# Query corner sums kept in PSUM, and a new order of DVE's steps in the attention units of a two-layer kernel

## The reference, cut to what matters

```python
q = rope(ln(x) @ Wq)        # 32 heads of 128
k = rope(ctx @ Wk)          # 8 heads of 128, four q heads share one
v = ctx @ Wv                # 8 heads of 128
s = 30 * tanh(q @ k.T * 0.0884 / 30)
w = softmax(where(mask, s, -1e30))
x = x + (w @ v) @ Wo
# rope(a) = a * cos + concat(-a2, a1) * sin, a1 and a2 the halves of 128
```

## Time and profile before

| what | us |
|---|---|
| median of 3 runs (lowest, highest) | 883.85 (883.29, 885.22) |
| the profiled execution, its own time | 885.6 |
| its span, first to last instruction | 883.8 |
| mean granted clock of PE | 0.986 |
| PE busy | 826.6 (94%) |
| DVE busy | 592.6 (67%) |
| ACT busy | 476.1 (54%) |
| POOL busy | 455.9 (52%) |

### The profile page before, as it was taken

How to read it: one execution, slowest core, us unless ns; L and a number is a source line. 1 busy time by engine, 2 the same in 40 slices (tenths; PEclk the granted TensorE clock), 3 DMA queues, 4 the chain that set the end, 5 groups by cost and what they waited for, 6 DMA issues and landing times.

```text
span 883.8 us, 12187 instructions
## 1 busy us (share of the span) xinstructions
PE 826.6 (94%) x4298; PEld 674.8 (76%) x4298; DVE 592.6 (67%) x1093; ACT 476.1 (54%) x1100; POOL 455.9 (52%) x341
## 2 busy tenths in 40 slices
PE   9999988689889988899888997999999999999998
PEld 7898866477667666677666775889998888888887
DVE  6873589667576785767857844647435766677894
ACT  6531334544555355543555523266778877877762
POOL 5564485755866768667686542011222432338442
PEclk9999999799999999999999998999999999999999
DMA  8364302302232222322221273000100110300002
GB/s 291 140 240 134 131 13 61 89 20 84 60 120 61 74 71 60 120 60 72 71 61 49 67 257 113 13 24 25 48 25 24 49 36 25 124 20 1 1 1 96
DMA packets 33245, 67.01 MB, mean 76 GB/s; under 512 B 5152, under 2 KB 8480, under 8 KB 32544
## 3 DMA queue, kind: packets, MB, share of 16 engines
q1 hardware_dynamic: 30640, 61.38, 22.3%
q10 hardware_dynamic: 2544, 4.85, 1.6%
HBM read 54.55 MB, written 11.67 MB: 75 GB/s over the span
## 4 chain that ended last, share of the span: by engine, by line
PE 52%; POOL 16%; DVE 14%; issue 10%; ACT 4%; DMA 4%; SPq 0%; DVEq 0%; POOLq 0%; ACTq 0%
PE PB L1790 10%; PE PB L1791 10%; PE PB L1792 10%; PE PB L2042 8%; PE PB L2057 3%; PE PB L1797 3%; PE PB L1827 2%; POOL WSl L1139 2%; POOL WVl L1139 2%; POOL W L1139 2%; DVE arena L1650 2%; POOL qb L1175 2%; DVE qb L1576 2%; POOL Eb L1195 2%; ACT arena L1312 2%
## 5 line engine op out<-in xcount | busy, mean ns | idle before, releaser
L1175 POOL TENSOR_TENSOR qb<-qb,arena 128x512 f32<-128x512 f32 x76 | 101.8, 1347 | 84.7 <-DVE arena L1583 44.3
L1476 DVE TENSOR_TENSOR xs<-xs,PB 128x512 f32<-128x512 f32 x111 | 74.1, 674 | 37.9 <-PE PB L1792 29.7
L1252 ACT ACTIVATE Oh<-PB 96x128 fp32r<-96x128 f32 (+2 forms) x236 | 79.3, 358 | 33.8 <-PE PB L1792 15.3
L1139 POOL TENSOR_TENSOR WVl<-stage,WVh 128x512 fp32r<-128x512 f32 (+1 forms) x25 | 37.4, 1513 | 70.7 <-ACT WVh L1252 64.3
L1790 PE MATMUL PB<-WVh,Oh 128*128 128x512 f32 x158 | 62.9, 398 | 5.6 <-POOL WVl L1139 5.3
L1827 PE MATMUL PB<-Th,WSh 128*128 128x512 f32 x112 | 45.7, 408 | 17.8 <-POOL WSl L1144 8.8
L1791 PE MATMUL PB<-WVl,Oh 128*128 128x512 f32 x158 | 61.6, 390 | 0.0
L1792 PE MATMUL PB<-WVh,Ol 128*128 128x512 f32 x158 | 61.6, 390 | 0.0
L1790 PE MATMUL PB<-W,Oh 128*128 128x512 f32 x142 | 56.5, 398 | 5.0 <-POOL W L1139 5.0
L1583 DVE TENSOR_TENSOR arena<-arena,ropeq 128x512 f32<-128x512 f32 x56 | 54.8, 979 | 4.3 <-ACT arena L1312 4.1
L1312 ACT ACTIVATE arena<-PB 64x512 f32<-64x512 f32 x28 | 16.5, 591 | 72.7 <-POOL qb L1175 70.5
(11 more groups left out here) (341 smaller groups left out, 2608.4 us busy)
## 6 DMA issues: line engine op xcount, KB each, us to landing
stage<-in_wq SPq DMA_DIRECT2D x44, 256.0 KB, 2.7
stage<-in_wo SPq DMA_DIRECT2D x44, 256.0 KB, 2.7
arena<-recs SPq DMA_DIRECT2D x32, 256.0 KB, 4.0
stage<-in_wk SPq DMA_DIRECT2D x12, 256.0 KB, 2.7
keys<-qb SPq DMA_DIRECT2D x12, 256.0 KB, 2.2
arena<-keys SPq DMA_DIRECT2D x6, 512.0 KB, 3.2
xs<-in_x SPq DMA_DIRECT2D x8, 256.0 KB, 6.9
ctx_hi<-cTh SPq DMA_DIRECT2D x1, 2048.0 KB, 8.8
```

The costliest lines, as they stand in the source:

```text
L1139: e.tensor_tensor(lo, src, hi.bitcast(f32), ALU.subtract).then_inc(s_wlo)
L1175: e.tensor_tensor(dst, dst, tmp, ALU.add).then_inc(s_radd)
L1252: return e.activation(dst, src, ACT.Copy)
L1476: e.tensor_tensor(xs[:, i, :], xs[:, i, :], PB[b][:, :], ALU.add).then_inc(free[b])
```

## The change

Three things are edited together.

1. The corner sums of the queries: `cmb` writes its sum into PSUM (bank 7 for t = 2 and 7, bank 0 for t = 3), not into `held`, and `rope p` becomes the three-instruction rope from PSUM that keys have. ACT's copies and the step `sin` are gone. Bank 7 is free only when rope 2 has read it. POOL's addition comes at the rope's place in the list.
2. The opening: the values' tiles go through `Eb` and `pTb` (`v_slot`), each two free for reuse when its transfer is done, no longer through `qb`; keys, values, q0 tiles, `pair(0)` and `pair(1)` stand in another order; the splits of wv0 1 stand ahead of the statistics.
3. The units: the addition of an output to x is a step of its own (`e0_add`), for units 0 to 13 moved behind output 2 and behind output 3. `sum0`, `norm0`, the splits of wp 2 and three of q0's tiles have other places in units 0 to 2, and `ctx_in` in unit 14.

```diff
 def e0(u, c, bank=None):
         stage("e0", u, c, bank=bank)
+        if u >= NU - 2:
+            e0_add(u, c)
...
     k0(5, 1)
     split("wk0", 7)
+    k0(6, 0)
+    spill_k(5, 1)
     vq(0)
-    spill_k(5, 1)
-    k0(6, 0)
+    spill_k(6, 0)
+    k0(6, 1)
     spill_v(0)
     split("wq0", 3)
     vq(1)
...
     spill_k(6, 1)
     k0(7, 0)
-    spill_v(2)
-    vq(3)
+    spill_v(1)
+    pair(0)
+    k0(7, 1)
     spill_k(7, 0)
...
+    for n in range(4):
+        vq(n + 2)
+        if n == 0:
+            spill_k(7, 1)
+            split("wq0", 2)
+        else:
+            spill_v(n + 1)
+        q0(0, n)
+        if n == 3:
+            q0(1, 1)
+    vq(6)
+    spill_v(5)
+    q0(1, 0)
+    q0(1, 3)
+    vq(7)
+    spill_v(6)
     spill_v(7)
     pair(1)
...
+        def added(*cs):
+            if u >= 2:
+                for c in cs:
+                    e0_add(u - 2, c)
...
+        if u == 1:
+            for n in range(2):
+                split("wp", u + 1, n)
         if u < 3:
             products(u, 1, 2)
-            query(0)
+        if u == 2:
+            step("sum0", 1)
+            step("sum0_out", 1)
+        if u == NU - 2:
+            step("ctx_in", 0)
         burst(u)
...
-        query(3)
-        if u in (1, *range(3, NU)):
+        if u >= 3:
             norm0(u - 1)
...
             products(u, 5)
             rope_p(u, 0)
-            sin(u, 0)
-        if u not in (1, 2):
+        if u >= 3:
             step("sum0", u)
             step("sum0_out", u)
         outputs(0)
-        if u >= NU - 2:
-            step("ctx_in", u - NU + 2)
-        query(1)
         if quad:
             products(u, 6, 3)
             rope_p(u, 1)
-        if 0 < u < NU - 3:
-            for n in range(2):
-                split("wp", u + 1, n)
+        if paired:
+            if u == 1:
+                step("pair", u + 1)
+            else:
+                for n in range(2):
+                    split("wp", u + 1, n)
         outputs(1)
         if quad:
             products(u, 7)
-            sin(u, 1)
-            query(2)
+            if u == 0:
+                q0(1, 2, bank=1)
             rope_p(u, 2)
-            sin(u, 2)
+        if u == 1:
+            norm0(0)
         if u == 2:
+            outputs(2)
+            added(0, 1)
             norm0(1)
-        if u in (1, 2):
-            step("sum0", u)
-            step("sum0_out", u)
-        outputs(2)
+            added(2)
+            step("sum0", 2)
+            step("sum0_out", 2)
+        if u != 2:
+            outputs(2)
+        if u == NU - 2:
+            step("ctx_in", 1)
+        if u != 2:
+            added(0, 1)
         if quad:
             products(u, 4)
             rope_p(u, 3)
-            sin(u, 3)
-        if 0 < u < NU - 3:
+        if u == 0:
+            step("sum0", 0)
+            step("sum0_out", 0)
+        if paired and u > 1:
             step("pair", u + 1)
         outputs(3)
+        added(*((3,) if u == 2 else (2, 3)))
...
# POOL: its addition for the queries
-                    if kind == "sin":
-                        pool.wait_ge(s_sin, 4 * k[0] + k[1] + 1)
+                    if k[0] == "p" and k[2] == 0:
+                        pool.wait_ge(s_sin, k[1] + 1)
                     else:
-                        pool.wait_ge(*read(*k))
+                        pool.wait_ge(*read(*product_of(*k)))
...
# ACT: rope p is removed
-                elif kind == "rope" and k[0] == "p":
...
-                    for r in range(2):
-                        last = e.activation(tmp_of(n)[64 * r:64 * r + 64], src[64 - 64 * r:128 - 64 * r], ACT.Copy, scale=-1.0)
-                    last.then_inc(s_swap)
...
# DVE
-                    cos = e.tensor_tensor(dst, src.rearrange("p (b t) -> p b t", b=8), ropeq[:, 0:1, :].broadcast_to([128, 8, 64]), ALU.mult)
...
-                    e.tensor_tensor(tmp, tmp, ropeq[:, 1:2, :].broadcast_to([128, 8, 64]), ALU.mult).then_inc(s_sin)
...
                     kept = held[{2: 1, 3: 6, 7: 5}[t]]
+                    to = PB[bank_of("p", u, 3 if t == 3 else 2)]
...
-                    e.tensor_tensor(kept, PB[bank_of("p", u, t)][:, :], kept, ALU.add).then_inc(s_cmb)
+                    e.tensor_tensor(to[:, :], PB[bank_of("p", u, t)][:, :], kept, ALU.add).then_inc(s_cmb)
```

More of the change, by code:

```diff
@@ L230, in plan @@
     stage("many")
+    split("wv0", 1, 0)
+    split("wv0", 1, 1)
     for i in HI:
@@ L846, in program @@
         s_spill = [sem(f"spill{n}") for n in range(8)]
+        s_vspill = [sem(f"vals_out{n}") for n in range(4)]
         s_kin, s_vin, s_cout, s_cin = [sem(f"keys_in{n}") for n in range(2)], sem("vals_in"), sem("ctx_out"), [sem(f"ctx_in{h}") for h in range(2)]
@@ L919, in products_of @@
             return x_block(((xTh, xTl), (Th, Tl))[kind], kk, hf)
-        spills = {st: n for n, st in enumerate(s[1:] for s in steps if s[0] == "spill")}
+        spills = {st: n for n, st in enumerate(s[1:] for s in steps if s[:2] == ("spill", "k"))}
         def spill_slot(*name):
@@ L934, in spill_done, with v_slot, v_sent, product_of @@
             return s_spill[n % 8], 16 * (n // 8 + 1)
+        def v_slot(i):
+            return (Eb, pTb)[i % 4 // 2][:, i % 2, :]
+        def v_sent(i):
+            return s_vspill[i % 4], 16 * (i // 4 + 1)
+        def product_of(kind, *k):
+            if kind != "p":
+                return (kind, *k)
+            u, t = k
+            return "p", u, (2, 5, 2, 1)[t]
         def tmp_of(n):
@@ L1165, in gpsimd_program @@
                     e.tensor_tensor(lo, wk0_1, hi.bitcast(f32), ALU.subtract).then_inc(s_k1lo)
-                elif kind == "sin" or kind == "rope" and k[0] != "p":
-                    name = ("p", *k) if kind == "sin" else tuple(k)
-                    n = ropes[name]
-                    dst = rope_place(*name)
+                elif kind == "rope":
+                    n = ropes[tuple(k)]
+                    dst = rope_place(*k)
                     tmp = tmp_of(n).rearrange("p (b t) -> p b t", b=8)
-                    if kind == "sin":
-                        pool.wait_ge(s_sin, 4 * k[0] + k[1] + 1)
+                    if k[0] == "p" and k[2] == 0:
+                        pool.wait_ge(s_sin, k[1] + 1)
                     else:
-                        pool.wait_ge(*read(*k))
+                        pool.wait_ge(*read(*product_of(*k)))
                     e.tensor_tensor(dst, dst, tmp, ALU.add).then_inc(s_radd)
@@ L1344, in scalar_program @@
                     act.wait_ge(*done("vq", i))
-                    if spills["v", i] >= 8:
-                        act.wait_ge(*spill_free("v", i))
-                    move(spilled[:, spill_slot("v", i), :], PB[b][:, :]).then_inc(free[b])
+                    if i >= 4:
+                        act.wait_ge(*v_sent(i - 4))
+                    elif i < 2:
+                        act.wait_ge(*done("xT", 0, 7))
+                    else:
+                        act.wait_ge(*done("many"))
+                    move(v_slot(i), PB[b][:, :]).then_inc(free[b])
                 elif kind == "b0":
@@ L1352, in scalar_program @@
                         act.wait_ge(*done("d0", u - 2, 1, 1))
-                    elif u == 0:
-                        act.wait_ge(*done("xT", 0, 7))
-                    else:
-                        act.wait_ge(*done("many"))
+                    else:
+                        for i in range(2 * u + 4, 2 * u + 6):
+                            act.wait_ge(*v_sent(i))
                     for h in range(2):
@@ L1611, in vector_program @@
                     dst = rope_place(*k)
+                    if k[0] == "p":
+                        _, u, t = k
+                        dve.wait_ge(*done("b0", u, 1))
+                        if t < 3:
+                            dve.wait_ge(s_cmb, 3 * u + t + 1)
+                        else:
+                            dve.wait_ge(*done("p", u, 4))
+                    else:
+                        dve.wait_ge(*done(*k))
                     dve.wait_ge(s_tab, 16)
-                    dve.wait_ge(*done(*k))
                     if k[0] == "k0":
@@ L1632, in vector_program @@
                     e.tensor_tensor(tmp[64:128], src[0:64], table[0:64, 1:2, :].broadcast_to([64, 8, 64]),
-                                    ALU.mult).then_inc(free[b])
+                                    ALU.mult).then_inc(s_sin if k[0] == "p" and k[2] == 0 else free[b])
                 elif kind == "keep":
```

72 lines of the change are left out of this document (14 added, 58 removed).

## The result

The changed kernel takes 836.03 us (median of 4 runs, 834.95 to 838.21), the kernel before 884.54 beside it (4 runs, 883.29 to 885.92). The ratio is 0.9454, 95% interval 0.943 to 0.9479. The forecast was 842.4, its range 831 to 859.

What follows compares the result with a forecast made beforehand. PE was taken as close to full almost everywhere, so only its gaps could be won. Gains of 10 (opening), 26.5 (steady units) and 5 (end), 41.5 in all, off the median 883.85 gave 842.4 us, range 831 to 859.

Steps and rivals of the forecast that it cites:

- The steady units: Units 4 to 13: a pair of units falls from 55.6 to 50.3 us, a gain of 26.5 us over five pairs.
- the contended 51.8: Steady units if POOL stays slowed by DVE's SBUF reads: 51.8 us a pair; as a rival 852 us, chance 0.20.
- the uncontended 49.1: Steady units if DVE's new ropes no longer slow POOL: 49.1 us a pair, without a wait before wo0.
- Rival 3: Gap-free: steady units at 49.1 us a pair gain 32.5, opening 14, end 8; 829 us, chance 0.12.
- ACT: Steady units: ACT's query copies stand 46.7 us, nearly all for POOL, delaying splits behind them; removing them saves ACT 4.9 a unit.
- Contention: Steady units: ropes with one PSUM input delay POOL no more; its wsum pieces fall from 1.19 towards 0.74 us.
- The PSUM write: Corner sums on DVE writing a whole PSUM bank: 0.68 us taken, bounds 0.68 and 1.56, three a unit.
- Rival 2: DVE becomes the bound, with more instructions and PSUM writes at the upper price: 54 us a pair, 865 us, chance 0.12.
- The opening: Units before the steady stretch: PE's waits fall from 18.7 to 14.3 us and the clock loss shrinks; gain 10, bounds 4 to 16.
- the 4 + 1.6: Clock part of the opening's 10 us gain, beside 4.4 from waits; clock loss before was put at 5 us.
- The end: End of the units: unit 14's record returns in about 3 us instead of 9.30; gain 5, bounds 0 and 9.
- Rival 4: Slower: bank 7, held until rope 2 is done, stops PE before each output 3; 894 us at 5.9 waits, chance 0.04.

Runs made afterwards that it cites:

- ctx_late: Changed kernel with the second half of the context loaded behind b0 of unit 15 instead of behind output 2 of unit 14: 832.59 us, 0.9407 of the kernel before.
- act_copies_back: Changed kernel with eight activations a unit put back on ACT, writing a tile that nothing reads: 836.79 us, 0.9447 of the kernel before.
- rope_from_held: Changed kernel with the three corner sums back in SBUF and ropes 0 to 2 reading them there: 873.58 us, 0.986 of the kernel before.
- wv0_late: Changed kernel with the two splits of wv0 for pair 1 back behind the statistics and k0(1,1): 839.37 us, 0.9473 of the kernel before.
- ctx_old: Changed kernel with both halves of the context loaded behind output 0 of units 14 and 15, as before: 839.77 us, 0.9481 of the kernel before.

## Why the prediction was right, and where its terms were off

The forecast of 842.4 is 6.4 us above the measured 836.03, which lies in the range and at the very edge of its middle part, 836 to 849. All three terms were too small, by 5.2, 2.0 and 1.0 us: 41.5 where the spans differ by 49.7.

**The steady units: right in mechanism, 5.2 us too small.** The term was 26.5, the measurement 31.7. The step that was off is the choice of 50.3 us a pair, about midway between the contended 51.8 and the uncontended 49.1 (exactly midway is 50.45). The pair is 48.86, below the lower end. What I held against the uncontended case, `norm0`'s two SBUF inputs beside wo0's splits, is there (W takes 1792 ns), but in nine of the ten units PE waits for none of it. That the splits start early enough is how I read this; ctx_late's unit 4 shows a case in which it does not suffice. Rival 3 described the stretch; its 32.5 is 0.8 from the measurement. I gave it a chance of 0.12, because it asked for all three terms at their best.

**ACT.** The prediction read ACT's long waits as the reason that the splits behind them came late. act_copies_back says that ACT's load and its waits for DVE are harmless. The same rows do show a likelier harm: 46.7 us of them are for POOL, and DVE waited for those copies. The 4.9 us a unit that ACT lost bought nothing.

**Contention.** This was weighed from two pieces of wsum, and its sign was right: with the sums in SBUF the ten units are up to 21.3 us longer. But the rotation's 25.7 us are not divided by any run between the shorter work of DVE and POOL and the end of DVE's waits for ACT and POOL. That the second counts is seen from rope_from_held: it has the long products, and more of them than the kernel before, and its ten units are still 277.95 - 267.59 = 10.4 us shorter, of which the deferred adds may be some. The sum took DVE's total as unchanged, 8.4 against 8.4; its busy time grew slightly, 201.7 to 207.2.

**The PSUM write.** Bounds 0.68 and 1.56, taken 0.68; measured 0.694 and 0.666. Rival 2, DVE as the bound, needed the upper price. DVE at 84% held nobody.

**The opening: 10 forecast, 12.0 measured.** The waits, forecast and measured: x sums 2.2 and 1.84; products 6 and 3 1.5 and 0.74; p2(1) 1.7 and 1.59; p4(1) 3.3 and 3.20; bank 4 0.7 and none; p5(2) 2.3 and 2.52; p1(3) 1.7 and 1.34; p5(3) 0.9 and 0.78. The sum is 14.3 against 12.0, nearly all in place and size. What was left out lies ahead of all of them: the splits of wv0, listed in the diff and given no term, end a wait of 1.77 us of PE at 38 us (wv0_late). The clock of the stretch to unit 4 rose from 0.92 to 0.96, as forecast. That the total came so near is in part luck. From the two rows of the first stretch, PE's idle time fell by 18.66 - 12.43 = 6.2 us, where 4.4 were forecast, and its busy time by 85.94 - 80.14 = 5.8. Of the latter 11 fewer matmuls, done ahead of 118.5, are about 2.5 (an estimate, at 0.228 each); the other 3.3 stand against the 4 + 1.6 that the forecast gave to the clock and its fall. No row showed the 1.6, and no run isolates it.

**The end: 5 forecast, 6.0 measured.** The record comes back in 4.17, not 3, and the wk1 load slowed to 5.87, both beside the early half, as the forecast feared; the 6.38 stayed, as 6.34. ctx_old gives the term by itself, 6.5. Its make-up was only half foreseen: PE's idle time in the rest fell from 9.46 to 5.91 us, 3.6, and its busy time by 2.4, with a granted clock in the first 60 us of the rest of 0.94 before and 1.00 after. The forecast had no term for the clock here.

**Rival 4, the slower case.** It put the danger at bank 7. That never showed. The real one was in the order: without the new rotation it makes each unit 2 us longer, by one long wait for a deferred add and the clock that falls with it. The prediction priced the order only together with the rotation and never apart.

## What to carry to other kernels

Where an intermediate is read several times by DVE while POOL works in SBUF, try leaving it in PSUM: in the ten units three products from PSUM took 83.3 us of DVE's instructions, where the two old ones took 85.9, and POOL's own work got shorter, 173.5 us instead of 192.5. Before moving work behind a step, ask what that step waits for: the same new order saved 5.9 us where DVE's ropes waited for no copy that itself waits for POOL, and cost 20 where they did. And give every moved line of a diff a term; two moved splits took away a wait of 1.8 us that the sum did not have.

## What the runs showed of the hardware

- The same idle time of PE can come with busy times that differ by 20 us. The ten units with 25.8 us of it, in waits of at most 1.4, ran at a granted clock of 1.00 with 252.2 us busy; those with 25.7 us, 25.5 of it in ten waits of up to 3.6, ran at 0.93 with 272.2.
- The clock also differs between executions of the same stretch. The changed kernel's unit 2 has 0.93 and takes 25.95 us; in wv0_late the same steps have 1.00 and take 24.26, and in ctx_old, whose program is the same from the start up to there, 24.23. That is 1.7 us, the size of several differences looked for here.

Unit 2 in the changed kernel, then in wv0_late:

```profile
157.50:183.45 25.95, 23.43 (x112) 18.22 (x111) 19.21 (x30) 7.29 (x12) 17.61 (x15) 0.93 0.26 72
```

```profile
159.54:183.80 24.26, 21.82 (x111) 17.08 (x110) 19.13 (x30) 7.30 (x12) 17.63 (x15) 1.00 0.27 77
```

- A DVE product of 128x512 from one tile, `part`, takes 1073 ns on the mean and from another, `part_u`, 692, with the same shapes; what POOL does at that moment differs. `part` is as fast when POOL is idle: in rope_from_held the product at 317.05 (L1648), after POOL's mask has ended at 316.49, takes 0.69 us, and the same instruction at 301.51, beside POOL's pieces of wsum, 1.13.
- A DVE product with both inputs in SBUF can be held up by several instructions of POOL in a row: `norm0` took 6.62 us in ctx_late's unit 4 and 2.03 in the changed kernel's.
